# Attention on Trainium2: ten position products spread over the late products, three copies given to ScalarE, a repeat set further back

## The reference, cut to what matters

```python
q = (h1 @ wq).reshape(b, l, H, DK)
k = (h1 @ wk).reshape(b, l, H, DK)
v = (h1 @ wv).reshape(b, l, H, DV)
basis = _rel_basis(l, N_POS)
qw = jnp.einsum('bihd,hdn->bihn', q, w_pos)
qr = jnp.einsum('bihn,ijn->bhij', qw, basis)
...
bias = (qr + uk + vr) * scale
scores = jnp.einsum('bihd,bjhd->bhij', q, k) * scale + bias
attn = jax.nn.softmax(scores, axis=-1)
out = jnp.einsum('bhij,bjhd->bihd', attn, v)
```

## Time and profile before

| | us |
|---|---|
| median of 3 runs | 1006.21 |
| lowest and highest | 1001.24, 1008.29 |
| the profiled execution | 1011.46 |
| its span | 1009.70 |
| attention phase, image by image | 318 to 415, 415 to 514, 514 to 613, 613 to 715 |
| TensorE busy in the span | 905.0 |
| VectorE busy in the span | 730.7 |
| ScalarE busy in the span | 646.9 |
| mean granted clock of TensorE | 0.949 |

### The profile page before, as it was taken

One profiled execution on the slowest core, in us unless ns is written; L12 is line 12 of the kernel. 1 busy time (PEld: TensorE's weight loads), 2 busy tenths in 40 slices (PEclk: granted clock), 3 DMA queues, 4 the chain that ended last, 5 costly groups with the idle time before them and its releaser, 6 DMA issues. The chain is left out here.

```text
span 1009.7 us, 20063 instructions
## 1 busy us (share of the span) xinstructions
PE 905.0 (90%) x6459; PEld 804.0 (80%) x6459; DVE 730.7 (72%) x1705; ACT 646.9 (64%) x1211; POOL 144.1 (14%) x204
## 2 busy tenths in 40 slices
PE   5999999999987889889988998898699996699996
PEld 5999999999985777667766776776498875599995
DVE  7899979979932786479657964887556334687785
ACT  4766757857724787579757975898444321766862
POOL 1000000000000143214421531144400000000000
PEclk9999999999987899999999999999779998699998
DMA  8003110179912686169616961695400030442201
GB/s 269 22 22 97 38 32 0 36 128 146 138 35 61 178 256 200 43 193 281 192 44 196 286 181 49 202 298 154 106 1 1 17 87 24 122 155 76 91 1 63
DMA packets 83799, 114.06 MB, mean 113 GB/s; under 512 B 12272, under 2 KB 44477, under 8 KB 83725
## 3 DMA queue, kind: packets, MB, share of 16 engines
q1 hardware_dynamic: 82636, 112.39, 41.1%
q10 hardware_dynamic: 1088, 0.79, 0.2%
HBM read 62.31 MB, written 47.67 MB: 109 GB/s over the span
## 5 line engine op out<-in xcount | busy, mean ns | idle before, releaser
L400 PE MATMUL psum<-w,feat 128*128 128x192 f32 x960 | 167.8, 330 | 13.6 <-ACT feat L330 10.1
L400 PEld LDWEIGHTS psum<-w,feat 128*128 128x128 f32 x960 | 156.5, 192 | 14.5 <-issue 10.0
L616 POOL TENSOR_SCALAR a_scores<-a_scores,a_inv 112x514 f32<-112x514 f32 (+1 forms) x160 | 113.0, 707 | 275.5 <-DVE a_inv L988 275.2
L973 DVE CUSTOM_DVE_ANT_0 a_scores<-psum,a_bias 112x514 f32<-112x514 f32 (+1 forms) x160 | 110.0, 688 | 50.1 <-PE psum L692 42.9
L845 ACT ACTIVATE a_scores<-a_scores,a_least 112x514 f32<-112x514 f32 (+1 forms) x160 | 116.7, 729 | 9.6 <-DVE a_least L973 8.3
L705 PE MATMUL psum<-ident,a_scores 112*112 112x112 f32 (+1 forms) x800 | 103.1, 261 | 14.6 <-DVE a_probsT L983 8.9
L418 PE MATMUL psum<-w_parts,parts 128*128 128x384 f32 x368 | 113.9, 374 | 2.5 <-DVE parts L232 2.3
L330 ACT ACTIVATE feat<-turn 128x1024 f32<-128x1024 f32 (+1 forms) x60 | 58.5, 974 | 85.1 <-DVE turn L215 52.4
L705 PEld LDWEIGHTS psum<-ident,a_scores 112*112 112x112 f32 (+1 forms) x800 | 78.1, 137 | 35.6 <-POOL a_scores L616 17.4
L692 PE MATMUL psum<-a_kh,a_q 128*112 128x258 f32 (+1 forms) x320 | 101.9, 339 | 1.0 <-DVE a_least L973 1.0
L420 PE MATMUL psum<-w_parts,parts 128*128 128x192 f32 x384 | 97.3, 253 | 0.0
(11 more groups left out here) (288 smaller groups left out, 1832.6 us busy)
## 6 DMA issues: line engine op xcount, KB each, us to landing
shear<-a_pos SPq DMA_DIRECT2D x128, 224.9 KB, 3.6
a_bias<-shear SPq DMA_DIRECT2D x128, 224.4 KB, 3.7
shear<-zero SPq DMA_DIRECT2D x20, 448.9 KB, 16.7
e_fc<-in_e_fc_dram SPq DMA_DIRECT2D x16, 384.0 KB, 3.8
x<-in_xT_dram SPq DMA_DIRECT2D x20, 256.0 KB, 3.0
e_proj<-in_e_proj_dram SPq DMA_DIRECT2D x8, 576.0 KB, 5.5
shear<-a_pos SPq DMA_DIRECT2D x32, 130.5 KB
a_bias<-shear SPq DMA_DIRECT2D x32, 130.3 KB
```

The costliest lines, as they stand in the source:

```text
L400: mm = pe.matmul(sums[m][:, 0:D], feat[:, r, j, 0, 128 * m:128 * m + 128], w[:, k, :], start=begins, stop=ends)
L616: pool.tensor_scalar(row, row, inv[0:TILES[g % NT][1], g % TT:g % TT + 1], 1.0, ALU.mult, ALU.mult).then_inc(weighed, 1)
L973: dve.tensor_tensor_reduce(halves(scores[0:r, g % TT, 0:PADL]), psum2(score_pair(g), r), halves(bias[0:r, g % MR, :]), -1.0 / 8, BIG, ALU. ...
```

## The change

The order and the sharing of work are changed, and nothing that is computed.

- `after_product` is now a written list, `BEHIND`. Before, positions 0 to 9 followed the halves (5, 0), (5, 1), (6, 0), (6, 1), (7, 0), (7, 1), (8, 0), (8, 1), (9, 0), (9, 1). Now position 3 and all behind it stand one half later: (7, 0), (7, 1), (8, 0), (8, 1), (9, 0), (9, 1), (10, 0).
- `by_vector`: VectorE copied the odd positions from 5 on. Now it copies 4, 6 and 8, and the odd ones from 13 on. So ScalarE copies 5, 7, 9 and 11, VectorE 4, 6 and 8; in all ScalarE has 23 copies in an image and had 22, VectorE 17 and had 18.
- ScalarE's repeat of k3 stands behind `weigh(3)`, not `weigh(0)`; VectorE's behind `add_bias(4)`, not `add_bias(2)`.

```diff
@@ attention_phase
-    SHARED = 4
...
-    by_vector = lambda g: g > SHARED and g % 2 == 1
-    vector_parts = lambda n: max(0, (n - SHARED) // 2)
+    by_vector = lambda g: g in (4, 6, 8) or g > AHEAD + 2 and g % 2 == 1
+    vector_parts = lambda n: sum(by_vector(g) for g in range(n))
     scalar_parts = lambda n: n - vector_parts(n)
...
-    after_product = lambda n, w: [g for g in [2 * (n - EARLY) + w - 2] if 0 <= g < AHEAD]
+    BEHIND = ((5, 0), (5, 1), (6, 0), (7, 0), (7, 1), (8, 0), (8, 1), (9, 0), (9, 1), (10, 0))
+    after_product = lambda n, w: [g for g, place in enumerate(BEHIND) if place == (n, w)]
...
                     weigh(g)
-                    if g == 0:
+                    if g == 3:
                         repeat(b, NP - 1)
...
                         add_bias(g)
-                    if g == 2:
+                    if g == 4:
                         repeat(b, NP - 1)
```

## The result

The changed kernel takes 998.73 us (median of 20 runs, 994.24 to 1463.47; one run far off the rest is left out of the ratio). The kernel before, in the same session, takes 1002.46 us (20 runs, 997.11 to 1010.7). The ratio is 0.9951, with a 95% interval of 0.9927 to 0.9974: 4.9 us faster, between 2.6 and 7.3 (the two medians as they stand differ by 3.7). The forecast was a gain of 4.6 us.

The account below looks back on a forecast made before the run. TensorE, VectorE and ScalarE are all nearly full in the loop, and ScalarE is late at the first tiles. Three images at 1.2 us plus 1.0 for the first give 4.6 us: 1006.21 to 1001.6 us, range 997.0 to 1008.5.

Parts of the forecast that it names:

- The late products: Before tile 0: q1's 1.1 us head start lost to position 9's copy; TensorE, ScalarE gain 0, VectorE 0.4 to 0.5 us.
- The first tiles: Exponential 0 to 6: position 12 freed of VectorE's copy 11, k3 repeats moved back; 1.2 us gained per image.
- One sign that I had set: At the first tiles: the forecast is wrong if TensorE idles over a microsecond for put 1.
- The clock: First tiles: the fall to 0.50 goes with the 1.63 us gap; if it stays, 0.8 us per image is left.
- the forward list: Instruction times worked forward through the first tiles: ScalarE's exponential 6 starts at 456.1 us, where it started at 457.28.
- The cross-check: ScalarE, exponential 0 to 6: 1.9 us of idle time, less the added copy of 0.48, leaves at most 1.4 us.
- The first image: VectorE waits for the store instead of ScalarE, exponential 0 at 343.95, then 9.8 us against 11.1: 1.0 us gained.
- The sum: Whole kernel: 3 × 1.2 + 1.0 = 4.6 us gained, to 1001.6 us; chance 0.48 for 3.8 to 5.5 us.
- That the clock still falls: Rival at the first tiles: remaining gaps keep the fall; gain 3.1 us, to 1003.1 us; chance 0.18.
- That the loop gives the head start back: Rival in the score-tile loop: a ring of waits sets its pace; gain 0, 1006.2 us; chance 0.12.
- That copy 9 comes late for its store: Rival in the late products: copy 9 waits for position 5's store to land; up to 1009.4 us; chance 0.11.
- More gain: Rival: all 1.9 us of ScalarE's idle and VectorE's 0.45 us gained, 9.2 us in all, 997.0 us; chance 0.11.

Follow-up runs that it names:

- places alone: Kernel after with position 11 back on VectorE and both k3 repeats at their old tiles; only positions 0 to 9 and copies 4 to 9 changed: ratio 0.9969.
- filler: Kernel before plus twelve extra matmuls, results unused, between score tile 2 and position 12: exponential 0 to 6 takes 10.04 us, ratio 0.9976.
- repeats not moved: Kernel after with both repeats of k3 back at tiles 0 and 2: exponential 0 to 6 takes 10.50 us, ratio 0.9984.
- VectorE's back: Kernel after with VectorE's repeat of k3 back at tile 2, ScalarE's still behind tile 3: ratio 0.9954.
- tile 25: Kernel after with both repeats of k3 behind tile 25: exponential 0 to 6 takes 8.49 us, ratio 0.9941.
- split: Kernel after with ScalarE's repeat of k3 as two single heads behind tiles 24 and 26, VectorE's whole repeat at tile 25: ratio 0.9942.

## Why the prediction was right

**The late products: right, with one thing missed.** TensorE and ScalarE gain nothing: q3 is held for the copy of position 9, and comes 12.32 us behind position 2 (before 12.21). Its matmuls start 10.27 us behind position 2 in both kernels (predicted 10.2). With the repeats later, score tile 0 comes 0.9 us sooner and exponential 0 0.37, which confirms the cause. Missed was what VectorE's lead is worth. I had it at 0.4 to 0.5 us at k3 and called VectorE's saving "not the term"; with the other two parts it brings exponential 1 from 2.06 to 1.56 us behind exponential 0, and the kernel with places alone is faster (through position 12).

**The first tiles: right, with two readings off.** Position 12 is issued 1.35 us behind exponential 0 (predicted 447.7 − 446.33 = 1.37), and put 1 stands right behind the repeat. Without the clock I had 0.8 us an image; with no fall on either side it is 0.66 (9.38 against 10.04 in the kernel with filler). One sign that I had set for the forecast being wrong did come: TensorE idles over a microsecond for put 1, 1.08 us at tile 2's transposes. It cost nothing here, since these transposes end at 449.20 and ScalarE, the late engine, comes to put 2 only at 449.30; 0.1 us was the margin, so the sign was badly chosen rather than the forecast safe. And minimum 6, which I put "a second ahead" (a microsecond: 455.1 against 456.1), is done at 450.9 against exponential 6 at 451.34, 0.4 us ahead; VectorE had less to spare than I wrote.

**The clock: right that it goes, and the term that was mis-sized.** I priced the fall at 0.4 us an image; it costs 0.9 by the filler, and by the two images of one kernel 0.76 at exponential 6 and 0.87 in the period. More than half of the gain is the clock's. In the forward list, which holds no fall, what was too long is ScalarE's pace: exponential 2 was to follow exponential 0 by 2.92 us and does by 2.75, exponential 3 by 4.12 and does by 3.79, exponential 6 by 9.8 and does by 9.38. I let an exponential hold ScalarE for 0.82 us ahead of a copy and it is 0.72 (441.96 to 442.68), a put for 0.38 and it is 0.32 (445.43 to 445.75). The cross-check, "all that may be saved of it, less the copy of 0.48, is 1.4 us", took those handoffs as fixed, and 1.57 went. Per image the gain is 1.55 us by the period, not 1.2.

The reason I gave, that the fall goes because the 1.63 us gap goes, is borne out by the table over the kernels and by the filler. The Trainium skill (TensorE: Matmul & The Clock Gate, "A second HAM failure mode: psum-queue depth-cycling") tells of a kernel whose frequent short idle times between groups of matmuls make the clock go up and down. Taken as a rule here, by which the short gaps left would keep the fall, it did not hold for the changed kernel with its gaps of 0.27 to 1.10 us. Three images of other kernels did fall behind such short gaps.

**The first image: right, in part by luck.** Timeline of VectorE after, and of ScalarE:

```profile
327.32 0.69 DVE L963 COPY a_pos<-psum 65x514 f32<-65x514 f32 x1 [4.05 <-DMA shear<-a_pos]
...
343.93 0.73 ACT L845 ACTIVATE a_scores<-a_scores,a_least 112x514 f32<-112x514 f32 x1
...
353.31 0.74 ACT L845 ACTIVATE a_scores<-a_scores,a_least 112x514 f32<-112x514 f32 x1
```

VectorE waits for the store, and 9.38 us follow exponential 0: a gain of 11.09 − 9.38 − 0.29 = 1.4 us, with 1.0 predicted. That exponential 0 comes at 343.93, where 343.95 was predicted, is luck: in the executions of five other kernels with the same late products (places alone, repeats not moved, VectorE's back, tile 25, split) it lies anywhere from 341.74 to 344.38, as the first stores land sooner or later.

**The sum.** By the profile it is 3 × 1.55 + 1.4 = 6.1 us (taking the last image, where a store holds the loop, as the others; there exponential 0 to 6 is 1.37 shorter); the runs measure 4.9 [2.6, 7.3]. The difference is within the interval, and may be the waits for stores in the loop: the profile after has one of 1.32 us in the last image, and every profile has one or several, at changing tiles. Nothing ties them to the change. So it is luck that the measured 4.9 lies so close to the forecast 4.6: the clock's term was half its size, the order's a little too large, and the interval would hold both sums. The predicted 1001.6 us lies 2.9 above the measured median because the kernel before ran at 1002.46 us in that session and not at 1006.21.

**The rivals.** That the clock still falls: no. That the loop gives the head start back: no, the loop takes the same time and the period is shorter by what the first tiles gained. That copy 9 comes late for its store: not once, in any profile here. More gain: by the profile a third of what that rival had above the forecast came.

## What to carry to other kernels

Where several engines hand tiles round, look at what stands ahead of a needed instruction in its engine's queue: moving a copy to another engine brought little alone, and moving an unneeded cast back a loss, because one edit left the wait that the other was to end. So price such parts by taking them out of the whole. Read the granted clock of each image for every such edit: here the clock had 0.9 us of an image, and the order of the instructions itself 0.66. A few matmuls whose results nothing uses, put into the wait, tell the clock's share from the rest, and may be worth keeping.

## What the runs showed of the hardware

At the first tiles the granted clock fell to 1.2 GHz for some 3.4 us (6.8 in three images) behind waits of TensorE of no more than 1.73 us, and three times behind waits of no more than 1.04 us, while another image of the same program with the same waits to 0.02 us kept 2.4 GHz. Such a fall costs 0.9 us of a period of 99 (99.47 against 98.55, 98.94 against 98.07), though the other engines' instructions keep their durations (an exponential 0.72 to 0.73 us at either level). Eight to twelve small matmuls in the wait (1.09 and 1.53 us) kept the clock up in all eight images of two kernels.

By the trace ScalarE starts its next instruction about 0.1 us before a copy out of PSUM ends (one of 0.59 us holds it for 0.48, one of 0.42 for 0.32). What an exponential of 0.73 us holds it for depends on what follows: 0.72 us ahead of a copy, 0.84 ahead of a cast.
